# Routed experts: eight tiles' expert numbers per register read on TensorE, in place of one per tile

## The reference, cut to what matters

```python
def _L1_ffn_ref(x, router_w, shared_gate, shared_up, shared_down, w_gate, w_up, w_down):
    B, S, H, I, E, NS, TOPK = (2, 256, 512, 352, 8, 1, 2)
    ...
    weights = jax.nn.softmax(logits, axis=-1)
    top_w, top_idx = jax.lax.top_k(weights, TOPK)
    comb = jnp.zeros_like(weights).at[jnp.arange(N)[:, None], top_idx].add(top_w)
    xb = flat.astype(jnp.bfloat16)
    ...
    ge = jnp.einsum('nh,eih->nei', xb, wg)
    ue = jnp.einsum('nh,eih->nei', xb, wu)
    he = jax.nn.sigmoid(ge) * ue
    de = jnp.einsum('nei,ehi->neh', he, wd)
    routed = (comb.astype(jnp.bfloat16)[:, :, None] * de).astype(jnp.float32).sum(axis=1)
    return x + shared_out.reshape(Bs, Ss, Hs) + routed.reshape(Bs, Ss, Hs)
```

## Time and profile before

| | |
|---|---|
| time, three runs | 1555.25, 1556.9, 1559.05 us, median 1556.9 |
| the profiled execution | 1555.22 us, of which the span is 1553.5 |
| busy | TensorE 1475.8 us (95%), weight loads 1074.8, VectorE 987.2, ScalarE 613.9, GpSimd 473.9 |
| the loop over tiles | from about 1417.7 to 1518.1 us of the span |
| granted TensorE clock | 0.986 of full speed over the span, 1.00 in the loop |

### The profile page before, as it was taken

One profiled execution on the slowest core, in us unless ns is written; L12 is line 12 of the kernel. 1 busy time (PEld: TensorE's weight loads), 2 busy tenths in 40 slices (PEclk: granted clock), 3 DMA queues, 4 the chain that ended last, 5 costly groups with the idle time before them and its releaser, 6 DMA issues. The chain is left out here.

```text
span 1553.5 us, 22540 instructions
## 1 busy us (share of the span) xinstructions
PE 1475.8 (95%) x7696; PEld 1074.8 (69%) x7696; DVE 987.2 (64%) x1905; ACT 613.9 (40%) x1085; POOL 473.9 (31%) x378
## 2 busy tenths in 40 slices
PE   7999889999999999999999999999999898998996
PEld 6788778788888888888887764444444376776554
DVE  6888987845545554553332757777777377567664
ACT  5243355613412431342221135555555635342554
POOL 1233433303421440441342222222222255004760
PEclk9999999999999999999999989999999899999999
DMA  6022347504311430334257683667662655733336
GB/s 216 28 82 79 129 156 247 176 11 144 100 54 41 151 102 4 122 95 164 97 179 227 202 224 105 176 189 196 189 196 101 238 188 187 265 131 129 106 96 230
DMA packets 105228, 223.39 MB, mean 144 GB/s; under 512 B 9328, under 2 KB 35312, under 8 KB 104240
## 3 DMA queue, kind: packets, MB, share of 16 engines
q1 hardware_dynamic: 101392, 211.96, 42.3%
q0 software_dynamic: 3744, 10.23, 2.1%
HBM read 157.54 MB, written 64.36 MB: 143 GB/s over the span
## 5 line engine op out<-in xcount | busy, mean ns | idle before, releaser
L1992 ACT ACTIVATE at_pt<-at_st 128x512 f32<-128x512 f32 (+3 forms) x384 | 164.5, 497 | 147.3 <-PE at_st L2024 146.2
L958 POOL TENSOR_TENSOR ff_w_lo<-ff_raw,ff_w_hi 128x1024 fp32r<-128x1024 f32 x64 | 155.7, 2433 | 206.6 <-ACT ff_w_hi L988 206.6
L115 PE MATMUL op_bank<-ff_x_hi,ff_w_lo 128*128 128x512 f32 x512 | 199.9, 390 | 0.5 <-issue 0.5
L116 PE MATMUL op_bank<-ff_x_lo,ff_w_hi 128*128 128x512 f32 x512 | 199.8, 390 | 0.0
L117 PE MATMUL op_bank<-ff_x_hi,ff_w_hi 128*128 128x512 f32 x512 | 199.7, 390 | 0.0
L1225 DVE TENSOR_TENSOR ff_h_lo<-ff_hf,ff_h_hi 128x512 f32 (+1 forms) x64 | 148.6, 2322 | 53.5 <-ACT ff_h_hi L1113 53.2
L2024 PE MATMUL at_st<-mx_qp,mx_kp 98*128 98x512 f32 (+3 forms) x288 | 104.5, 395 | 13.9 <-ACT at_pt L1992 10.5
L988 ACT ACTIVATE ff_w_hi<-ff_raw 128x1024 fp32r<-128x1024 f32 x64 | 67.8, 1061 | 118.3 <-PE op_bank L117 116.2
L115 PEld LDWEIGHTS op_bank<-ff_x_hi,ff_w_lo 128*128 128x128 f32 x512 | 96.5, 188 | 21.2 <-issue 0.9
L117 PEld LDWEIGHTS op_bank<-ff_x_hi,ff_w_hi 128*128 128x128 f32 x512 | 96.4, 188 | 20.4
L116 PEld LDWEIGHTS op_bank<-ff_x_lo,ff_w_hi 128*128 128x128 f32 x512 | 96.4, 188 | 20.2
(11 more groups left out here) (460 smaller groups left out, 3341.1 us busy)
## 6 DMA issues: line engine op xcount, KB each, us to landing
ff_raw<-in_Wug SPq DMA_DIRECT2D x64, 512.0 KB, 3.6
at_raw<-in_expert_gu SPq DMA_DIRECT2D x16, 704.0 KB, 12.2
mx_qp<-q_hi SPq DMA_DIRECT2D x12, 512.0 KB, 6.4
mx_kp<-k_hi SPq DMA_DIRECT2D x12, 512.0 KB, 11.3
at_raw<-in_expert_d SPq DMA_DIRECT2D x8, 768.0 KB, 13.8
expert_gu_bf<-at_cast SPq DMA_DIRECT2D x16, 352.0 KB, 10.8
ex_e_gu<-expert_gu_bf SPq DMA_DIRECT2D x8, 704.0 KB, 8.4
tm_ln_res<-in_x SPq DMA_DIRECT2D x4, 1024.0 KB, 5.5
```

Of the source, the lines that this page charges most:

```text
L115: pe.matmul(out, cut_l(ll), cut_r(rh), start=first, stop=False, **kw)
L116: pe.matmul(out, cut_l(lh), cut_r(rl), start=False, stop=False, **kw)
L958: pool.tensor_tensor(w[j][1][:, :, :, :], raw[:, j], f32(w[j][0][:, :, :, :]), ALU.subtract)\
L1992: act.activation(pt[:, s % PT, h, off:TB], st[(s * HG + h) % ST][:, off:TB], ACT.Exp, scale=SCALE).then_inc(exp_done, 1)
```

## The change

```diff
+    OWNERS = 8
...
-        def expert_of(q):
-
-            return pe.value_load(owner[0:1, q:q + 1], min_val=0, max_val=EXPERTS - 1)
+        def experts_of(q):
+
+            _, values = b.nc.values_load_multi_w_load_instructions(owner[0:1, q:min(q + OWNERS, TILES)], [mybir.EngineType.PE],
+                                                                   min_val=0, max_val=EXPERTS - 1)
+            own.update(enumerate(values, q))
...
-        own = {0: expert_of(0)}
+        own = {}
+        experts_of(0)
         turn_x(0)
         turn_x(1)
         for q in range(TILES):
             gate_up(q, own[q])
-            if q + 1 < TILES:
-                own[q + 1] = expert_of(q + 1)
+            if q + 1 < TILES and (q + 1) % OWNERS == 0:
+                experts_of(q + 1)
             if q >= 1:
                 turn_he(q - 1)
```

## The result

The changed kernel takes 1559.16 us (median of 20 runs, 1557.01 to 1562.39), the kernel before on the same chip 1556.03 (20 runs, 1552.26 to 1559.44): a ratio of 1.0017, 95% interval 1.0009 to 1.0025. The change costs some 3 us by the medians (1.4 to 3.9 by the interval); the forecast was a gain of 2.9. The profiled execution of after has a span of 1557.6 us against 1553.5, and a granted clock of 0.984 against 0.986.

The account below looks back on a forecast made before the run. POOL's 2.57 us a tile bounds the loop, TensorE's step being about as long. First send 1.17 earlier, less 0.4, plus 2.1, less 0.15, plus 0.20: 2.9 gained, 1556.9 to 1554.0 us; range 1552.4 to 1559.8.

Parts of the forecast that it names:

- The read's price: A read of eight closes TensorE's queue for 0.72 us plus seven further registers, 3.17 in all.
- u: Cost of one more register in a read: 0.15 us of load plus 0.20 of register work and check, 0.35.
- Rival 1: The load pays in full for each register, 0.30 us; TensorE becomes the bound, 2.9 us slower, 1559.8; chance 0.10.
- rival 3: The call makes one load and check per register, queue closed for 5.76 us; 6.3 slower, 1563.2; chance 0.05.
- The steps without a read: TensorE's loop steps that lose their read take 2.25 us, 0.32 shorter than the mean step of 2.57.
- The first send: POOL's first send, behind three early reads, comes 1.17 us earlier, and its whole chain with it.
- The first hole: TensorE idles 2.0 us at the first large read in the loop; POOL waits 0.4 at `send(5)`.
- The cover of 1.2: TensorE's queue runs about 1.2 us ahead, hiding that much of each large read and leaving a hole of 2.0.
- rival 2: TensorE's clock falls to half for 10 us behind two of four holes; 7 us slower, 1564; chance 0.10.
- The sum's frame: Per eight tiles TensorE needs 20.0 us and POOL 20.56, so POOL's 2.57 a tile sets the pace.
- However cheap the read, 3.4 at most: Largest possible gain, with a hole of 0.2: 1.17 + 2.2 - 0.15 + 0.20 = 3.4 us.
- Two bounds of one length: In the loop POOL takes 2.57 us a tile and TensorE's step, 2.51 with a read, is about as long.

Follow-up runs that it names:

- e13: The changed kernel with eight fetches ahead of the first send in place of six and five output rows in place of three; ratio 0.9987 to the kernel before.
- e6: The changed kernel run again, unchanged; ratio 1.0020 to the kernel before.
- e7: The changed kernel (reads of eight) without the bounds check; ratio 0.9991 to the kernel before.
- e11: Single reads, one per tile as in the kernel before, but without the bounds check; ratio 0.9985 to the kernel before.
- e8: The changed kernel with one load of eight, but each value's check where its single read had stood; ratio 0.9996 to the kernel before.
- e14: e7 (reads of eight, no check) with eight fetches ahead in place of six and five output rows in place of three; ratio 0.9964 to the kernel before.
- e15: e11 (single reads, no check) with eight fetches ahead in place of six and five output rows in place of three; ratio 0.9963 to the kernel before.
- f17: e8 (checks spread) with eight fetches ahead in place of six and five output rows in place of three; 1548.84 us, ratio 0.9951 to the kernel before.
- the first group: Four disturbed variants of the changed kernel: no check, checks spread, reads of four, eight fetches ahead; ratios 0.9994, 0.9996, 0.9986, 1.0008 to the kernel before.
- f16: The kernel before with eight fetches ahead in place of six and five output rows in place of three; ratio 0.9996 to the kernel before.
- e9: The changed kernel with reads of four in place of eight, checks kept; ratio 0.9998 to the kernel before.
- e10: e7 (reads of eight, no check) with eight fetches ahead of the first send in place of six; ratio 0.9981 to the kernel before.
- e5: The kernel before run again, unchanged; ratio 0.9998 to the kernel before.
- e12: The kernel before with eight fetches ahead of the first send in place of six; ratio 0.9990 to the kernel before.

## Why the prediction was wrong, step by step

- **The read's price: right in sum, wrong in its parts.** The load takes 0.045 per further register on the average, not 0.15; the check 0.28, not 0.20. 0.33 in place of u = 0.35, and the queue closed for 3.05 in place of 3.17. Rival 1 (the load pays in full, 0.30) and rival 3 (one load per register) are refuted by five load rows with a median of 0.61. The rule of the Trainium skill (Runtime: NRT & Kernel Launch, Instruction fetch mechanics), 200 ns a register even in bulk, does not hold for this load from on-chip memory: 0.31 for seven more.
- **The steps without a read: right.** 2.24 us on TensorE (2.25), a gap of 0.15.
- **The first send: right.** 15.18 to 14.01, 1.17 earlier as forecast, and 1.1 to 1.2 in every kernel with reads of eight or four.
- **The first hole: right.** 2.17 less the 0.15 of the pace is 2.0, as forecast, with the clock kept; GpSimd waited 0.24 longer at `send(5)` (idle 0.54 less its usual 0.30), where 0.4 had been forecast.
- **The cover of 1.2, carried over to the later holes: the step that failed.** Found: 3.05 less 2.02 = 1.0 at the first, and 0.2, 0.4 and 0.6 at the others (the last with its queue closed for 3.2). The prediction had both halves in its own text: that TensorE would come to wait for the fetches (at most 2.2 ahead), and that the cover is the time by which the queue runs ahead. It did not put them together: an engine that has just waited for data has a queue that waits as well, with nothing issued ahead (ahead of the second read the weight load of `turn_x` had waited 1.15). The gain on TensorE ended where it used up its own cover. e13 shows it: without fetch waits the cover is about 1.0 at all four (0.9 to 1.05).
- **The clock: rival 2, given 0.10, is by an estimate most of the loss.** It said holes of 2.0 to 2.9 us, and falls at two of four; there were three, behind holes of 2.6 to 2.8. Its price was too high: the earlier trace rows gave 10 us at half the clock, here it is 3.4, 1.4 of the array and 0.8 of the loop. At 0.8 each three falls are, as an estimate, some 2.3 of the 3.0 us; e6 has two and is 0.8 shorter. By the same estimate the loop would still be some 0.7 longer than before without any fall, so the clock alone did not turn the sign: the longer holes did it with the clock. No run has three such holes without a fall.
- **The sum's frame: right until TensorE became late.** GpSimd's 2.57 a tile did cap the gain. But eight steps of TensorE came to 8 x 2.24 + 2.8 = 20.7 at the second hole, and 1.4 for the clock on top, against 20.56: GpSimd waited at each large read, 4.6 in all beyond its usual 0.30 where the working had 0.4, four of its operations took 1.1 longer in all, its first send was 1.17 early, and its last fetch moved by the balance, from 96.2 to 100.6. From there to the last send it is 12.3 in place of 13.8; 4.5 - 1.5 = 3.0.
- **"However cheap the read, 3.4 at most": about three times what a cheap read brought.** e7 and e11 made the read nearly free and gained 1.1 to 1.2 in the loop. In e7 the 1.17 of the early first send are gone by the last fetch (96.2, as before): GpSimd waited for nobody in between, but four of its operations took 1.09, 1.15, 1.39 and 1.48 in place of 0.97 to 0.99, 1.2 together. From the last fetch to the last send it gained 13.8 - 12.6 = 1.2, where the working had 2.1. This second term was mis-sized by one row: `fetch(38)` was said to land 2.8 after its start, which is the median of all fetches. The view of line L2454 for that fetch alone, in before, says:

```profile
DMA to landing us min/median/max: 3.9/3.9/3.9
```

So `turn_x(38)`, 5.06 behind the fetch, had 1.2 to gain and not 2.2; in after, e7, e8, e11, e14, e15 and f17 it starts 4.0 to 4.2 behind the last fetch.
- **The measured time lies inside the stated range by luck.** 1559.2 is near the 1559.8 at which rival 1 set the range's end, but rival 1's slow load never came; other causes, put outside of the range or at nothing, led there.
- **Two bounds of one length: right, with one figure off.** TensorE's own step with a read is 2.57 on the average and not the 2.51 of the one step in the earlier trace rows; what the sum takes from that step, the 2.25 without a read, is right.
- **Behind the loop: right.** Last send to end is 33.7 in both.

What stays open: what decides, beside its length, whether an idle stretch of 1.9 to 2.5 us is followed by the lower level; what stretches single operations of GpSimd; why the last load is slow; and what stretched the first group's loop.

## What to carry to other kernels

A batch of reads gathers their checks as well: split a read into load and check before batching, take the loads together and leave each check in the step that used to hide it. A stall that is covered by an engine's lead is covered only as long as the engine leads: once it waits for somebody else's data, price the next stall without cover, and ask whether the clock may fall behind it. Read the landing of the one transfer that sets the end, not the median. And where two bounds of one length run side by side, test each by relieving it alone: in the loop, relieving one gave 0 (f16) or 1 us (e7), both and the third behind them 5.5 (f17).

## What the runs showed of the hardware that I had not expected

- A register load from on-chip memory costs 0.30 us for one register, 0.33 for four (e9) and 0.61 for eight, but 1.01 for the last three in e9 and 1.07 for the last seven in after; a check of one value closes TensorE's queue for 0.28 us, though its two rows (0.15 and 0.02) show only 0.17 of it.
- Equal idle stretches of TensorE (1.86 us, after and e13) had the granted clock at 1.00 behind one and at 0.50 behind the other; 2.29 and 2.53 kept it (e6, e10), 2.44 and 2.65 did not (after). Each fall in the loop lasted 3.4 us.
- A fetch or send on GpSimd takes 0.97 to 1.00 us as a rule. Where TensorE ran irregularly, one to six of them took 1.2 to 1.5 (the 1.30 in f17's rows above); before, e5, e12 and f16 have none but the first fetch. What delays them is not known. In e7 they ate the whole 1.17 that the early first send had won.
